# Edge numbers transposed on TensorE instead of scattered by DMA, and a last group of one chunk, in a four-layer graph kernel

## The chip, the cores and the metric

The kernel runs on one core of one Trainium2 chip. The metric is device time in microseconds (us). It is one launch that computes four graph layers over the same 3125 nodes and 53125 edges. The engines are PE (TensorE), DVE (VectorE), ACT (ScalarE), POOL (GpSimd) and SP (SyncE); each works through its own instructions in order and waits on semaphores. SP issues nearly all the plain DMAs, POOL the indirect ones (gathers of rows by an index list).

## The reference, cut to what matters

```python
# x: (3125, 256); src, dst: (53125,) int32, sorted by dst; edge_weight: (53125,)
x = layernorm(x + relu(segment_sum(norm * (x @ W0)[src], dst) + b0))            # layer 0
x = layernorm(x + segment_sum(w * x[src], dst) @ Wrel.T + b + x @ Wroot.T)      # layer 1
z = einsum('nd,hdf->nhf', x, W)                                                 # layer 2, 4 heads of 64
es, ed = (z * a_src).sum(-1), (z * a_dst).sum(-1)
e = leaky_relu(es[src] + ed[dst], 0.01);  e = where(e == 0, -1000, e)
m = segment_max(e, dst);  ex = exp(e - m[dst]);  alpha = ex / segment_sum(ex, dst)[dst]
x = layernorm(x + segment_sum(alpha[:, :, None] * z[src], dst).reshape(N, 256))
x = layernorm(x + relu(segment_sum(w * (x @ W3)[src], dst) + b3))               # layer 3
```

The change concerns how layer 2 reads `src` and `dst`. Both are 212.5 KB lists of integers in memory.

## The kernel before, in words

**Layers 0, 1 and 3** work by tiles of 128 nodes (25 tiles). For 16 of them ("dense") a weighted adjacency matrix is built from one-hot matrices and multiplied on PE; for the other 9 ("sparse") POOL gathers source rows and PE scatters them. To find the edges of a tile, the kernel writes an edge list to memory (`tab` to `flat`, L464), and from it a table `etab` of overlapping rows of 128 edges (L474, 4983 KB); POOL gathers 32 of these rows per dense tile (`edge_rows`, L642, into `raw`).

**Layer 2** works by groups of 640 consecutive edges: 128 partitions times KC = 5 chunks. There are 84 groups; 83 are full, and the last has 5 edges. For each group POOL issues 5 indirect DMAs, each gathering 128 rows of `ztab` by the indices `idx[:, g, c]` (L706). DVE builds the one-hot of destinations from `dstf[:, g, c]`, forms the logits, maxima and exponents with ACT, and PE sums prob times rows in 4 heads times 5 chunks (L1872, 20 matmuls, which the profile shows as 40). The groups form a software pipeline: in one iteration g DVE takes logits of g+1, maxima of g and rescales g-2; PE sums group g-1.

**The edge layout in layer 2.** Partition p of group g holds the 5 consecutive edges 640g + 5p to 640g + 5p + 4. So loading `dst` to `dst_i[p, g, k]` (L470) and copying `src` to `source_nodes[p, g, k]` in memory (L475) go in pieces of 5 integers (20 bytes): 128 times 83 of them each. The last group has 1 partition with 5 edges; its other partitions get node 0 from a small zeroed tile `spare` (L478) and a destination of 1e30 (L922).

**The order of work at the start.** SP issues from one instruction stream: the first edge loads (L445 to L447, which wait for DVE's clearing memsets through s_pad), x, the weights, the edge list, three padded copies of the lists, then the destinations (L470, L472), `etab` (L474, after the edge list), the sources (L475 to L478), the 25 tiles of layer 0's rows in five stores (L482, each behind five tiles of the loop below), and then the index lists of the first sparse blocks (L502). DVE meanwhile makes digit one-hots (L1002, L1003) that PE counts (L1523) into degrees (L1061), and after that DVE, ACT and PE run **the x loop**: 25 tiles, each turned on PE (L1550), copied by ACT (L734), multiplied (L1558), scaled by ACT (L729), split in bf16 parts by DVE and ACT (L1093, L745, L1086). At tile 23 DVE first needs the gathered `raw` rows (L992). After the loop DVE makes the first one-hots of layer 0 (L1118 to L1126), then waits for the list of destinations of the first sparse block (L1179), and adds the first weights (L1139); from there on the layers run as one long chain.

POOL waits for `etab`, gathers `raw` (L642), clears two tiles by memset (L667), and goes on with the gathers of layer 0.

Of the kernel before, what the change touches and what calls it, by code (L numbers as in the profile page):

```python
# [7 lines left out]
ALU = mybir.AluOpType  # L8
# [31 lines left out]
NOWHERE = 4095  # L40
WIDE = 18
# [6 lines left out]
def gnn_program(nc, x, src, dst, edge_weight, w0, b0, w_rel, b_rel, w_root, w_att, att, w3, b3, out):  # L48
# [6 lines left out]
    REST = (E - FULL * EP * KC) // KC  # L55
# [8 lines left out]
    assert FULL * EP * KC + REST * KC == E and 0 < REST < EP  # L64
# [73 lines left out]
    landed_between = [16 * KC * len(range(s, GROUPS, SLOTS)) for s in range(SLOTS)]  # L138
# [7 lines left out]
    with ctx:  # L146
# [48 lines left out]
        spare = sb("spare", [EP, KC], I32)  # L195
# [29 lines left out]
        def carver(whole):  # L225
# [38 lines left out]
        dst_i = carve(EP, FULL + 1, KC, dt=I32)  # L264
# [11 lines left out]
        ybuf = big2[:, 0:2 * NPAD].rearrange("p (t f) -> p t f", f=D)  # L276
        aw = [big2[:, (2 + j) * NPAD:(3 + j) * NPAD].rearrange("p (b d) -> p b d", b=NT) for j in range(2)]
# [69 lines left out]
        sparse1_banks, sparse3_banks = banks[2:4], banks[0:2]  # L347
        granules = banks[7][0:1, 3 * NPAN:3 * NPAN + NT]
# [91 lines left out]
        def _(sp):  # L440
# [276 lines left out]
        def _(act):  # L717
# [53 lines left out]
            for h in range(2):  # L771
                digits(0, h, first=True)
# [742 lines left out]
        def _(pe):  # L1515
# [447 lines left out]
```

## Time and profile before

| | us |
|---|---|
| median of 3 runs (1622.21 to 1625.48) | 1622.26 |
| the profiled execution's own time | 1624.98 |
| its span on the core | 1623.2 |
| PE busy | 1440.8 (89%) |
| DVE busy | 1172.5 (72%) |
| POOL busy | 900.7 (55%) |
| ACT busy | 487.2 (30%) |

The span is some 1.8 us shorter than the execution's own time, which holds what lies around it. The page also gives the chain of waits that ended last: PE has 48% of it, POOL 16%, "issue" 12%, DVE 9%, DMA 9%, SP's queue 3%. Two of its entries lie in one stretch at the start (the table `edge_rows` and the gather from it), and POOL's 15% is layer 2, where L706 issues 420 gathers. In the timeline a row has its start, its length, the engine and line, the tiles out<-in, and in brackets the idle time before it and who ended that.

### The profile page before, as it was taken

How to read it: one execution, taken by the hardware profiler on the slowest of the kernel's cores; microseconds unless marked ns; L12 is line 12 of the kernel's file. 1: busy time of each engine (PE TensorE's matmuls, PEld its weight loads, DVE VectorE, ACT ScalarE, POOL GpSimd, SP SyncE). 2: the span in 40 equal slices, each digit the busy share in tenths (PEclk: the TensorE clock that was granted, in tenths of full speed). 3: DMA queues.
4: the chain of work that ended last, by engine and by line, in shares of the span. 5: the costliest groups of instructions: out<-in, count | busy, mean ns of one | idle time of the engine just before them, and what ended most of it. 6: DMA issues, size and time to landing. Idle time of an engine off the chain costs nothing.

```text
span 1623.2 us, 36636 instructions
## 1 busy us (share of the span) xinstructions
PE 1440.8 (89%) x12043; PEld 1162.8 (72%) x12043; DVE 1172.5 (72%) x3011; ACT 487.2 (30%) x907; POOL 900.7 (55%) x913
## 2 busy tenths in 40 slices
PE   4949999999998999999588898888888879999998
PEld 4738777877776888887366666666666657888887
DVE  9768888888863344345599999999999969443433
ACT  0522222222210111013355545455555546100000
POOL 0126455554454556563677777777777710456774
PEclk9969999999999999999599999999899969999999
DMA  8975545445565565541344444444444441766652
GB/s 203 109 155 173 166 163 181 143 163 165 195 218 208 183 200 189 171 142 47 94 111 112 114 111 112 112 114 111 113 113 111 112 138 66 262 209 226 199 152 80
DMA packets 132296, 241.49 MB, mean 149 GB/s; under 512 B 70299, under 2 KB 94975, under 8 KB 125967
## 3 DMA queue, kind: packets, MB, share of 16 engines
q0 software_dynamic: 45024, 128.68, 28.3%
q1 hardware_dynamic: 87087, 110.47, 22.9%
q8 instruction: 100, 1.64, 0.4%
q14 instruction: 85, 0.70, 0.1%
HBM read 193.42 MB, written 50.96 MB: 151 GB/s over the span
## 4 chain that ended last, share of the span: by engine, by line
PE 48%; POOL 16%; issue 12%; DVE 9%; DMA 9%; SPq 3%; ACT 1%; DVEq 1%; POOLq 0%
PE bank L1740 15%; POOL ring L706 15%; PE bank L1622 7%; PE bank L1688 7%; PE bank L1614 3%; PE bank L1667 3%; PE bank L1872 3%; PE bank L1640 3%; DMA edge_rows<-edge_list 2%; DMA ring<-attention_rows,work 2%; DMA big<-rows_layer,big 2%; PE bank L1749 2%; POOL big L661 1%; PE bank L1607 1%; DMA ring<-edge_rows,ring 1%
## 5 line engine op out<-in xcount | busy, mean ns | idle before, releaser
L706 POOL DMA_INDIRECT ring<-attention_rows,work x420 | 399.6, 951 | 150.4 <-issue 146.4
L661 POOL DMA_INDIRECT big<-rows_layer,big x304 | 289.6, 953 | 265.9 <-issue 241.2
L657 POOL DMA_INDIRECT ring<-rows_layer,ring x152 | 149.9, 986 | 181.7 <-PE bank L1667 131.7
L1872 PE MATMUL bank<-work,ring 128*65 128x48 f32 x3360 | 239.8, 232 | 9.3 <-ACT work L874 8.6
L1872 PEld LDWEIGHTS bank<-work,ring 128*65 128x65 f32 x3360 | 228.9, 148 | 18.2 <-ACT work L874 16.8
L874 ACT ACTIVATE work<-work 128x960 f32<-128x960 f32 x84 | 161.6, 1924 | 84.3 <-DVE work L1419 83.6
L1740 PE MATMUL bank<-big,ring 128*128 128x256 f32 x750 | 164.2, 379 | 0.0
L1740 PEld LDWEIGHTS bank<-big,ring 128*128 128x128 f32 x750 | 142.5, 190 | 19.5
L1740 PE MATMUL bank<-big 128*128 128x256 f32 x664 | 145.9, 379 | 0.0
L1688 PE MATMUL bank<-big 128*128 128x256 f32 x608 | 139.2, 383 | 7.4 <-DMA big<-rows_layer,big 7.2
L1740 PEld LDWEIGHTS bank<-big 128*128 128x128 f32 x664 | 126.1, 190 | 17.7 <-ACT big L898 0.4
L1622 PE MATMUL bank<-big 128*128 128x256 bf16 x1200 | 133.8, 273 | 0.6
L1688 PEld LDWEIGHTS bank<-big 128*128 128x128 f32 x608 | 114.0, 192 | 26.2 <-DMA big<-rows_layer,big 10.1
L1855 PE MATMUL bank<-ident 128*32 128x512 bf16 x420 | 130.4, 411 | 0.0
L1622 PEld LDWEIGHTS bank<-big 128*128 128x128 bf16 x1200 | 116.1, 98 | 16.2 <-ACT big L758 3.0
L1847 PEld LDWEIGHTS bank<-ident,work 96*128 96x128 f32 x336 | 46.4, 199 | 108.3 <-DVE work L1400 104.1
L1847 PE MATMUL bank<-ident,work 96*128 96x96 f32 x336 | 60.5, 305 | 65.0 <-DVE work L1400 64.4
L763 ACT ACTIVATE std<-mv,epsc 128x1 f32<-128x1 f32 x100 | 29.4, 294 | 288.8 <-DVE mv L1145 286.4
L1386 DVE TENSOR_TENSOR work<-work,bank 128x960 f32<-128x960 f32 x84 | 96.1, 1144 | 0.9 <-issue 0.8
L1126 DVE TENSOR_TENSOR work<-work,ring 128x1600 bf16<-128x1600 bf16 x102 | 96.1, 983 | 0.0
L1394 DVE TENSOR_REDUCE work<-work 128x192 f32<-128x960 f32 x84 | 96.0, 1143 | 0.0
L1419 DVE TENSOR_TENSOR work<-work,bank 128x960 f32<-128x960 f32 x84 | 95.8, 1141 | 0.0
(254 smaller groups left out, 2290.5 us busy)
## 6 DMA issues: line engine op xcount, KB each, us to landing
adjacency<-big SPq DMA_DIRECT2D x16, 1600.0 KB, 6.4
big<-adjacency SPq DMA_DIRECT2D x16, 1600.0 KB, 8.0
ring<-adjacency SPq DMA_DIRECT2D x16, 1600.0 KB
ring<-attention_rows,work POOLq DMA_INDIRECT x420
rows_layer<-big SPq DMA_DIRECT2D x50, 128.0 KB, 2.2
edge_rows<-edge_list SPq DMA_DIRECT2D x1, 4983.0 KB
big<-rows_layer,big POOLq DMA_INDIRECT x304, 2.9
rows_layer<-big SPq DMA_DIRECT2D x5, 960.0 KB, 10.8
```

Source lines behind the costliest of these rows:

```text
L657: G.indirect_dma_start(out=rows0[:, s, :], out_offset=None, in_=y0tab[:, :], in_offset=bass.IndirectOffsetOnAxis(ap=src_l0[j][:, c:c + 1], ...
L661: G.indirect_dma_start(out=rows1[:, s, :], out_offset=None, in_=(y1tab if q < 2 * LAYER else y3tab)[:, :], in_offset=bass.IndirectOffsetOn ...
L706: G.indirect_dma_start(out=rows[0:EP, s, c, 0:ZG], out_offset=None, in_=ztab[:, :], in_offset=bass.IndirectOffsetOnAxis(ap=idx[:, g, c:c + ...
L874: S.activation(prob[:, k % 2, :, :], val[:, k % 3].rearrange("p a c -> p c a"), ACT.Exp).then_inc(y["prob_ready"], 1)
L1126: ins = V.tensor_tensor(oh[h][2][:, j], oh[h][1], repeated(digs[h][:, W1 + j], NT * PAN), ALU.mult)
L1386: V.tensor_tensor(val[:, k % 3].rearrange("p (h w) c -> p h w c", h=H), pen[:, k % 3].unsqueeze(1).to_broadcast([EP, H, WIN, KC]), lg.rear ...
L1622: ins = mm(dense_bank[:, 0:D], ac[:, b, :], y0p[:, b, j, :], start=False, stop=False, skip_group_check=True)
L1688: mm(bank[:, 0:D], hot1[:, q % 2, c, :], rows1[:, s, :], start=False, stop=False, skip_group_check=True).then_inc(chunk_done, 1)
L1740: ins = mm(bank[:, 0:D], slots[s][:, b, :], ybuf[:, b, :], start=(b == 0), stop=(b == NT - 1), skip_group_check=True)
L1847: ins = mm(mb_bank[:, j * 2 * WIN:(j + 1) * 2 * WIN], mg[:, j:j + 1].to_broadcast([2 * WIN, P]), ident[0:2 * WIN, 0:2 * WIN], start=True, ...
L1855: mm(bank[0:32, :].rearrange("p (a b) -> p a b", a=4), ident16[:, 0:32], columns, start=True, stop=True, skip_group_check=True)
L1872: ins = mm(sum_banks[k % 3][0:FH, h * WIN:(h + 1) * WIN], rows[0:EP, s, c, h * FH:(h + 1) * FH], prob[:, k % 2, c, h * WIN:(h + 1) * WIN], ...
```

## The change

Sources and destinations are loaded with one group per partition: `dst_g` and `src_g` are 84 partitions of 640 consecutive edges (pieces of 2560 bytes), lying in the storage that layer 0's output rows take later. ACT casts both to float. PE transposes each in 5 blocks of 84x128 into bank 7, in the x loop's steps 4 (destinations) and 9 (sources). ACT copies the turned destinations to `dstf` in its step 4; DVE casts the turned sources to integers (`src_t`) in its step 13; SP stores `src_t` to `source_nodes` behind a wait for that. Edge c*128 + p of a group is now in chunk c and partition p. With that order the last group's 5 edges are all in chunk 0, so POOL gathers one chunk for it and PE sums one chunk. Some semaphores of the count phase are merged, and padded destinations are 2^24 in place of 1e30.

```diff
+            for a, d in ((dst_g, dst), (src_g, src)):
+                sp.dma_start(a[0:FULL, :], d[0:FULL * EP * KC].rearrange("(g e) -> g e", g=FULL)).then_inc(ld_dsti, 16)
+                sp.dma_start(a[FULL:GROUPS, 0:REST], d[FULL * EP * KC:E].rearrange("(g e) -> g e", g=1)).then_inc(ld_dsti, 16)
             sp.wait_ge(s_tab, 6)
             sp.dma_start(flat[0:P * COLS, :].rearrange("(p e) f -> p e f", p=P), tab[:]).then_inc(s_flat, 16)
...
-            sp.dma_start(dst_i[:, 0:FULL, :], dst[0:FULL * EP * KC].rearrange("(g p k) -> p g k", p=EP, k=KC)).then_inc(
-                ld_dsti, 16)
-            sp.dma_start(dst_i[0:REST, FULL, :], dst[FULL * EP * KC:E].rearrange("(p k) -> p k", k=KC)).then_inc(ld_dsti, 16)
             sp.wait_ge(s_flat, 32)
             sp.dma_start(etab[:, :], bass.AP(flat.tensor, 0, [[GRAN * FIELDS, ROWS + 1], [1, P * FIELDS]])).then_inc(s_etab, 16)
-            sp.dma_start(src_all[:, 0:FULL, :], src[0:FULL * EP * KC].rearrange("(g p k) -> p g k", p=EP, k=KC)).then_inc(
-                s_srcs, 16)
-            sp.dma_start(src_all[0:REST, FULL, :], src[FULL * EP * KC:E].rearrange("(p k) -> p k", k=KC)).then_inc(s_srcs, 16)
-            sp.dma_start(src_all[REST:EP, FULL, :], spare[REST:EP, :]).then_inc(s_srcs, 16)
+            sp.wait_ge(s_srct, 1)
+            sp.dma_start(src_all, src_t).then_inc(s_srcs, 16)
...
@@ POOL, layer 2
-                    for c in range(KC):
+                    for c in range(chunks_of(g)):
@@ ACT, before the degrees, and in its x loop
+            act.wait_ge(ld_dsti, 64)
+            S.copy(dst_gf, dst_g).then_inc(s_grows, 1)
+            S.copy(src_gf, src_g).then_inc(s_grows, 1)
...
+                if t == 4:
+                    act.wait_ge(s_gturn, 1)
+                    S.copy(dstf[:].rearrange("p g c -> p c g"), turned_numbers).then_inc(s_grows, 1)
...
@@ DVE, clearing at the start (before s_pad), and in its x loop
-            V.memset(spare[:], 0)
+            V.memset(dst_g[GROUPS // 32 * 32:GROUPS, :], FAR_NODE)
+            V.memset(src_g[GROUPS // 32 * 32:GROUPS, :], 0)
...
-            dve.wait_ge(ld_dsti, 32)
-            V.tensor_copy(dstf[:, 0:FULL, :], dst_i[:, 0:FULL, :])
-            link(V.tensor_copy(dstf[0:REST, FULL, :], dst_i[0:REST, FULL, :]))
...
+                if t == 13:
+                    dve.wait_ge(s_gturn, 2)
+                    V.tensor_copy(src_t.rearrange("p g c -> p c g"), turned_numbers).then_inc(s_srct, 1)
@@ PE, x loop and layer 2
+            def turn_numbers(of, ready):
+                pe.wait_ge(s_grows, ready)
+                for c in range(KC):
+                    ins = T(turned_numbers[:, c, :], of[:, c * EP:(c + 1) * EP], ident[0:GROUPS, 0:GROUPS])
+                ins.then_inc(s_gturn, 1)
...
+                if t == 4:
+                    pe.wait_ge(s_cur, 1)
+                    turn_numbers(dst_gf, 1)
+                elif t == 9:
+                    turn_numbers(src_gf, 3)
...
-                        for c in range(KC):
+                        for c in range(chunks_of(k)):
```

SP's stream before, from the edge list to layer 0's rows (`edge_rows` is `etab`, `rows_layer` the rows of layer 0, `big` on-chip storage):

```order
L464 DMA edge_list<-big 128x2496 [waits s_tab]
L465 DMA edge_list<-big 1x96
L470 DMA big<-in_dst 128x83x5
L472 DMA big<-in_dst 1x5
L474 DMA edge_rows<-edge_list 3322x768 [waits s_flat]
L475 DMA source_nodes<-in_src 128x83x5
L477 DMA source_nodes<-in_src 5x1
L478 DMA source_nodes<-spare 127x5
L482 DMA rows_layer<-big 128x5x768 [waits b_p3] x5
```

(The six padded copies, L468 and L469, stand between L465 and L470.) The same stretch now:

```order
L476 DMA big<-in_dst 83x640
L477 DMA big<-in_dst 1x5
L476 DMA big<-in_src 83x640
L477 DMA big<-in_src 1x5
L479 DMA edge_list<-big 128x2496 [waits s_tab]
L480 DMA edge_list<-big 1x96
L486 DMA edge_rows<-edge_list 3322x768 [waits s_flat]
L488 DMA source_nodes<-big 128x420 [waits s_srct]
L492 DMA rows_layer<-big 128x5x768 [waits b_p3] x5
```

The two loads moved ahead of the edge list, and the store of the sources stands alone behind `edge_rows`, with a wait.

PE's stream at the x loop's steps 3 to 5 before (`x_sb` is turned to banks 1 and 6, the products go to banks 4 and 5):

```order
L1550 MATMUL bank1<-ident,x_sb 128x128 [waits b_xTc]
L1550 MATMUL bank1<-ident,x_sb 128x128
L1558 MATMUL bank5<-ring,xnT 128x256 [waits b_r1,b_xTc]
L1558 MATMUL bank5<-ring,xnT 128x256
L1550 MATMUL bank6<-ident,x_sb 128x128 [waits b_xTc]
L1550 MATMUL bank6<-ident,x_sb 128x128
```

and now:

```order
L1568 MATMUL bank1<-ident,x_sb 128x128 [waits b_xTc]
L1568 MATMUL bank1<-ident,x_sb 128x128
L1576 MATMUL bank5<-ring,xnT 128x256 [waits b_r1,b_xTc]
L1576 MATMUL bank5<-ring,xnT 128x256
L1598 MATMUL bank7<-ident,big2 128x84 [waits s_grows,s_cur]
L1598 MATMUL bank7<-ident,big2 128x84 x4
L1568 MATMUL bank6<-ident,x_sb 128x128 [waits b_xTc]
L1568 MATMUL bank6<-ident,x_sb 128x128
```

Five transposes of the numbers stand between a product and the next turn of x; the sources' five stand in the same way five steps later.

## Rows read from the trace of the kernel before

**Rows 1.** Timeline, SP's DMA queue: start, length (us), line.
```profile
26.86 7.51 SPq L472 DMA_DIRECT2D big<-in_dst  x1
...
36.13 12.83 SPq L475 DMA_DIRECT2D source_nodes<-in_src  x1
49.00 40.83 SPq L477 DMA_DIRECT2D source_nodes<-in_src  x1
...
90.34 10.56 SPq L482 DMA_DIRECT2D rows_layer<-big  x5
103.36 0.39 SPq L502 DMA_DIRECT2D ring<-edge_sources  x1
```
**Rows 2.** The chain that ended last, from the start: start, length, what.
```profile
34.41 39.85 DMA edge_rows<-edge_list
...
75.31 19.95 DMA ring<-edge_rows,ring
```
**Rows 3.** Waits, 0 to 130 us: total us, times, longest.
```profile
DVE ring L992 <- DMA ring<-edge_rows,ring: 7.1, 1, 7.1
...
DVE deg L1061 <- PE bank L1523: 2.6, 1, 2.6
...
DVE ring L1179 <- DMA ring<-edge_destinations: 2.5, 1, 2.5
```
**Rows 4.** Timeline, DVE at the start, a clearing memset and the first work.
```profile
1.28 0.41 DVE L915 MEMSET big<- 32x417 int32 x1
...
5.79 0.38 DVE L940 TENSOR_SCALAR big<-big 128x416 int32<-128x416 int32 x1 [0.90 <-DMA big<-in_dst]
```
**Rows 5.** Windows in the x loop: us, busy per engine, clock, DMA share, GB/s.
```profile
64.00:74.00 10.00, 9.82 (x51) 7.70 (x49) 8.27 (x21) 8.70 (x26) 0.00 (x0) 1.00 1.40 14
```
**Rows 6.** Timeline, 56 to 82 us, durations of kinds of work.
```profile
56.00 1.09 PE L1575 MATMUL bank<-ident,ring 128*128 128x128 f32 x8
59.42 0.38 PE L1550 MATMUL bank<-ident,x_sb 128*128 128x128 f32 x2
65.08 0.68 DVE L1078 COPY w_rr<-bank 128x512 f32<-128x512 f32 x1
72.29 0.28 DVE L1068 COPY wz<-ring 128x256 f32<-128x256 f32 x1
76.33 5.48 POOL L667 MEMSET big<- 128x3200 f32 x2
77.31 0.42 DVE L1086 TENSOR_TENSOR big<-work,big 128x256 bf16<-128x256 f32 x1
80.32 1.65 DVE L1068 COPY wz<-ring 128x256 f32<-128x256 f32 x1
```
**Rows 7.** Timeline, the end of layer 2.
```profile
1304.18 0.95 POOL L706 DMA_INDIRECT ring<-attention_rows,work  x1 [0.30 <-issue]
1306.79 0.42 PE L1838 MATMUL bank<-ident,work 128*96 128x128 f32 x2
1309.47 0.18 DVE L1366 TENSOR_TENSOR work<-ring,bank 128x20 f32<-128x20 f32 x1 [3.08 <-DMA ring<-attention_rows,work]
1311.01 4.57 PE L1872 MATMUL bank<-work,ring 128*65 128x48 f32 x40
1317.09 0.42 DVE L1400 TENSOR_REDUCE work<-bank 96x2 f32<-96x256 f32 x1 [1.96 <-PE bank L1838]
1318.26 2.52 PE L1872 MATMUL bank<-work,ring 128*65 128x48 f32 x40
1322.45 3.62 PE L1872 MATMUL bank<-work,ring 128*65 128x48 f32 x40 [1.68 <-ACT work L874]
```
**Rows 8.** DMA issues: KB each, median us from issue to landing.
```profile
rows_layer<-big SPq DMA_DIRECT2D x5, 960.0 KB, 10.8
```
**Rows 9.** Windows, for the granted clock (third figure from the right).
```profile
112.00:120.00 8.00, 7.02 (x93) 6.69 (x94) 5.42 (x12) 2.81 (x7) 5.92 (x7) 0.58 0.43 125
...
1310.00:1312.00 2.00, 1.95 (x14) 1.95 (x14) 1.82 (x6) 0.00 (x0) 0.00 (x0) 0.50 0.01 4
```

More of the change, by code:

```diff
@@ L40 @@
 NOWHERE = 4095
+FAR_NODE = 1 << 24
 WIDE = 18
@@ L54, in gnn_program @@
     GROUPS = FULL + 1
-    REST = (E - FULL * EP * KC) // KC
+    REST = E - FULL * EP * KC
+    LAST_CHUNKS = -(-REST // EP)
     NT = -(-N // P)
@@ L63, in gnn_program @@
     MOST = -(-ROWS // (P // GRAN)) + 1
-    assert FULL * EP * KC + REST * KC == E and 0 < REST < EP
+    assert 0 < REST < EP * KC and GROUPS * KC <= 512
     assert GROUPS > 2 * SLOTS and SLOTS % 2 and NPAD - N >= WIN and D == 2 * P
@@ L137, in gnn_program @@
     landed_before = [landings(2 * TEN - SLOTS + s, 2) for s in range(SLOTS)]
-    landed_between = [16 * KC * len(range(s, GROUPS, SLOTS)) for s in range(SLOTS)]
+    landed_between = [16 * sum(KC if g < FULL else LAST_CHUNKS for g in range(s, GROUPS, SLOTS)) for s in range(SLOTS)]
     def list_loads(q):
@@ L276, in gnn_program @@
         ybuf = big2[:, 0:2 * NPAD].rearrange("p (t f) -> p t f", f=D)
+        carve = carver(big2)
+        dst_g = carve(GROUPS, KC * EP, dt=I32)
+        src_g = carve(GROUPS, KC * EP, dt=I32)
+        dst_gf = carve(GROUPS, KC * EP)
+        src_gf = carve(GROUPS, KC * EP)
+        src_t = carve(EP, GROUPS, KC, dt=I32)
         aw = [big2[:, (2 + j) * NPAD:(3 + j) * NPAD].rearrange("p (b d) -> p b d", b=NT) for j in range(2)]
@@ L358, in gnn_program @@
         s_digits, s_dup = sem("s_digits"), sem("s_dup")
-        s_gq, s_hist, s_histc, s_hT, s_colsum, s_colsumc, s_first, s_cur, s_nswb = (
-            sem(f"s_{n}") for n in ("gq", "hist", "histc", "hT", "colsum", "colsumc", "first", "cur", "nswb"))
-        s_srcs = sem("s_srcs")
+        s_gq, s_totals, s_totals_read, s_cur, s_nswb = (sem(f"s_{n}") for n in ("gq", "totals", "totals_read", "cur", "nswb"))
+        s_srcs, s_srct, s_grows, s_gturn = sem("s_srcs"), sem("s_srct"), sem("s_grows"), sem("s_gturn")
         s_tab, s_flat, s_etab = sem("s_tab"), sem("s_flat"), sem("s_etab")
-        s_gm, s_gmT, s_dg, s_bb, s_sweeps = (sem(f"s_{n}") for n in ("gm", "gmT", "dg", "bb", "sweeps"))
+        s_ranges, s_ranges_spread, s_sweeps = sem("s_ranges"), sem("s_ranges_spread"), sem("s_sweeps")
         s_onehots, s_cnt, s_deg, s_sqd, s_dinv = (sem(f"s_{n}") for n in ("onehots", "cnt", "deg", "sqd", "dinv"))
@@ L404, in has, with chunks_of, landed_rows @@
             return 0 <= g < GROUPS
+        def chunks_of(g):
+            return KC if g < FULL else LAST_CHUNKS
+        def landed_rows(r, g):
+            return r * landed_between[g % SLOTS] + 16 * (KC * (g // SLOTS) + chunks_of(g))
         def uses(r, g):
@@ L551, in _ @@
             sp.sem_inc(held, 1)
-            sp.wait_ge(s_srcs, 48)
+            sp.wait_ge(s_srcs, 16)
             sp.dma_start(idx, src_all).then_inc(idx_ready, 16)
@@ L772, in _ @@
                 digits(0, h, first=True)
+            act.wait_ge(s_srcs, 16)
             def rows_of_layer1(m):
@@ L921, in _ @@
             V.memset(pad_w, 0.0).then_inc(s_pad, 1)
-            link(V.memset(dstf[:, FULL:, :], BIG))
             V.memset(epsc[:], EPS)
@@ L1025, in _ @@
             link(V.tensor_scalar(rounds, rounds, float(P // GRAN), None, ALU.mult))
-            V.tensor_reduce(most[:], banks[7][0:1, 2 * NPAN:3 * NPAN], AX_X, ALU.max).then_inc(s_colsumc, 1)
-            dve.wait_ge(s_colsumc, 1)
+            V.tensor_reduce(most[:], banks[7][0:1, 2 * NPAN:3 * NPAN], AX_X, ALU.max).then_inc(s_totals_read, 1)
+            dve.wait_ge(s_totals_read, 2)
             link(V.tensor_tensor(most[:], most[:], unsorted[0:1, :], ALU.max))
@@ L1363, in logits_sum @@
                 def logits_sum(k):
-                    dve.wait_ge(gathered[k % SLOTS], 16 * KC * uses(r, k) + nswb * landed_before[k % SLOTS])
+                    dve.wait_ge(gathered[k % SLOTS], landed_rows(r, k) + nswb * landed_before[k % SLOTS])
                     dve.wait_ge(y["lg"], 5 * number(k) + 6)
```

43 lines of the change are left out of this document (21 added, 22 removed).

## The prediction

> **What bounds the kernel now.** I read the page's chain of waits first, then its pieces in order of time, because the change acts at two places only: the first 115 us and the last 25 us of layer 2. At the start the chain runs through SP's issues, then through the transfer that makes `edge_rows` (39.85 us) and the gather from it (19.95 us) [rows 2]. SP's queue shows why they are so long: the issue of the piecewise load of the destinations held SP 7.51 us, and the piecewise copy of the sources 12.83 and 40.83 us, until 89.83 [rows 1]. They are 128 x 83 pieces of 20 bytes each, issued around `edge_rows`, and the gather by POOL shares the DMA engines with them.
>
> What that costs is not 54 us. The table of waits gives what DVE lost by it: 7.1 us at L992 for the gathered rows, in the x loop's tile 23, and 2.5 us at L1179 for the first list of destinations [rows 3]. Everything else of the backlog lies beside DVE, ACT and PE, which work on counts and on the x loop until then. In the x loop PE is busy 9.82 of 10 us, ACT 8.70 and DVE 8.27 [rows 5]: the three are a ring with little room, and work put into it is paid nearly in full.
>
> In layer 2 POOL issues gathers without a pause, 0.95 us each and 0.30 between them, 1.25 us a chunk [rows 7]. DVE waits a little for each group. For the last group it waits 3.08 us, from 1306.39 [rows 7], since that group's five gathers ended at 1305.13. Behind it the pipeline drains: two groups of sums on PE, and the last one, with nothing beside it, 3.62 us.
>
> **The start, what goes.** (1) The wait of 7.1 us at L992. Now `edge_rows` has no pieces ahead of it or behind it. Even if its transfer took the old 39.85 us and the gather the old 19.95, counted from an issue some 5 us earlier (7.51 us of issue gone, about 2.5 added), they would end near 90, about when DVE arrives; without the pieces they end tens of microseconds earlier. I take all 7.1.
>
> (2) The wait of 2.5 us at L1179. SP issued the list at 103.36 because it had only come to the five stores of layer 0's rows at 90.34 and needed 10.56 us to issue them [rows 1], 960 KB each, which landed 10.8 us after issue [rows 8] with the list behind them. Now SP is free for the stores as the x loop delivers tiles, at tile 14, 15, 20 and 25, so one store is left at the end. The lists are then issued 2.5 us behind it (103.36 less 100.90), around 96. DVE has the 9 to 10 us of one-hots to do after its loop, so the list has landed. I take all 2.5.
>
> (3) POOL's two memsets (5.48 us from 76.33) lay in the x loop. DVE's copy L1068 took 1.65 us where its twin took 0.28, and ended with them; the sum L1086 beside them took its usual 0.42 [rows 6]. POOL comes to the memsets as soon as `raw` is gathered, now near 47, so the copy is free again: 1.37 us less. (The Trainium skill, "SBUF — State Buffer", section "Who interferes with whom", says that VectorE's two-port copies and a GpSimd instruction exclude one another for their whole length, while an operation with two on-chip inputs is held up only by a GpSimd instruction that reads. This trace agrees: 1.65 against 0.28, and 0.42 unchanged.)
>
> Together 10.97 us.
>
> **The start, what comes.** (4) Two memsets of 640 integers per partition before s_pad. At 0.41 us for 416 [rows 4] that is 0.63 each, 1.26 us. SP's first load waits for them, and DVE idled 0.90 us for that load's data [rows 4], so the delay goes into the path: +1.26. (5) PE's 2 x 5 transposes. Eight of 128x128 took 1.09 us, 0.136 each, and two of `x_sb` 0.38, 0.19 each [rows 6]; an 84-column one is no longer. From below PE might hide them in its 0.18 us of idle per 10, so nearly nothing; I take 10 x 0.136 = 1.36, bounds 0 and 1.9. (6) ACT's copy of 420 turned numbers, and DVE's cast of 420. The nearest row is 0.68 us for 512 from the same kind of bank [rows 6], so 0.56 each; between 0 (room in the ring) and 0.68. I take 1.12. (7) ACT's two casts of the untransposed numbers and the new loads lie in ACT's idle time before the degrees: nothing, if the loads are there by then (below, the rival that ends slower). (8) The two DVE casts into `dstf` go, but DVE waited 2.6 us for PE right behind them [rows 3]: nothing. (9) SP's new wait for DVE's step 13 has the store of the sources and all five row stores behind it. The first two of these come up to eight tiles later than they could, still some 20 us ahead of where they were; POOL's gathers need the last store only: nothing.
>
> (The Trainium skill, "TensorE: Matmul & The Clock Gate", Part 4 on the transpose mode, gives about 275 ns for a 128x128 bf16 transpose in a kernel. Ten of these would be an estimate of 2.75 us and take 1.4 us from the gain. The trace here has 0.136 to 0.19 for fp32, and the measurement decides.)
>
> Sum of costs 1.26 + 1.36 + 1.12 = 3.74; the start gains 10.97 - 3.74 = 7.2 us. Bounds: costs from 1.26 to 1.26 + 1.9 + 1.36 = 4.5, so 6.5 to 9.7. From there on all layers are one chain, and the whole is shifted.
>
> **The end of layer 2.** (10) The last group gathers once, so its data is there 4 x 1.25 = 5 us earlier, near 1304.4, and DVE does not wait at L1366. It could go on at 1306.39. But the next instruction, the group maximum, needs PE's L1838, which ended at 1307.21; it began about 0.1 us after L1366's 1309.47. So 1309.58 less 1307.25, 2.3 us, are gained; at most 3.08. (11) The sums at 1311.01 ran at a granted clock of 0.50 [rows 9], the lower level of 1.2 GHz, and took 4.57 us where the next 40 matmuls took 2.52 [rows 7]. By this the transposes came late and DVE waited 1.96 us at L1400 [rows 7]. PE is idle 2.3 us less ahead of them, and whether the clock is high then I can't tell: 0 to 1.96, I take 1.0. (12) The last group's sums are 4 matmuls in place of 20, 8 of the 40 in the row: 8/40 x 3.62 = 0.72, at the low clock 8/40 x 4.57 = 0.91. With nothing beside them 2.7 us go; at most 2.9.
>
> Together 2.3 + 1.0 + 2.7 = 6.0 us, bounds 5.0 and 7.9. The DVE and ACT work of the last group keeps its size.
>
> **Sum.** 7.2 + 6.0 = 13.2 us. The profiled execution took 1624.98 us, its span 1623.2, so it would take 1611.8 with a span near 1610.0. Against the median of the runs shown, 1622.26, that is 1609.1; I say 1609. The bounds alone give gains of 11.5 to 17.6, 1604.7 to 1610.8.
>
> **Rivals.**
>
> A. The memsets hit DVE at their new place. Near 47 to 53 DVE makes one-hots, which PE's counts and the degrees wait for. For it: L1068. Against it: L1086 with two inputs was untouched. If each waited as L1068 did, up to 5.48 us come back: 13.2 - 5.5 = 7.7, 1614.5.
>
> B. The end of layer 2 is bound by PE's and DVE's own drain. The wait at L1366 becomes one for PE, the low clock stays, and of (10) and (11) nothing is left: 7.2 + 2.7 = 9.9, 1612.4. Against it: L1838 was done at 1307.21.
>
> C. The clock is up where it was low. From 112 to 120 PE was busy 7.02 us at a mean granted clock of 0.58 [rows 9]; at full clock that work takes 4.1, so up to 2.9 us. With shorter idle stretches of PE before it, and the full 1.96 of (11), the gain is 13.2 + 2.9 + 1.0 = 17.1, 1605. Against it: PE still has about 5 us of nothing while DVE makes the first one-hots.
>
> D. Slower than before. ACT takes its instructions in order, and its two casts wait for all four new loads before it may take the square root of the degrees, near 56.5 (PE's work behind the last count starts at 56.00 [rows 6]). Nothing of the x loop starts without it. Each microsecond that the loads land after that is one lost. If they landed as late as `edge_rows` did, at 74.3 [rows 2], the loss is 17.8, less the 13.2: 1622.26 + 4.6 = 1626.9. It decides from 56.5, and outweighs the gains from about 70. For it: a load queued behind 3 MB of x and the weights. Against it: 84 pieces of 2560 bytes, ahead of the edge list, not behind it.
>
> E. The change doesn't do what it says: the gather is late by itself, for instance since `edge_rows`, 3322 rows of overlapping reads, is what takes long, or the list waits for SP all the same. By (1) even the old durations leave little of the wait; but if both waits stayed, the start would lose 3.74 - 1.37 = 2.4 us, and with the 6.0 of layer 2's end the whole gain would be 3.6; with the low bound of 5.0 there it is 2.6, no change by measurement: 1619.7.
>
> **How the numbers follow.** My forecast 0.66; A 0.10; B 0.08; C 0.10; D 0.03; E 0.03. A change of 0.2%, 3.2 us, is about what a measurement of this kernel can tell from none. Faster than that are the forecast, A, B and C: 0.94; E is the same, 0.03; D is slower, 0.03. The range goes from C with the top of its bounds, 1602.5, to A, 1614.5; the forecast's own is 1604.7 to 1610.8.
>
> **What the profile after would show.** SP's queue with no issue over 2 us between `edge_rows` and the row stores; L992's and L1179's successors without a wait on a DMA; the memsets near 47 and one-hots of 0.57 and 0.68 us beside them; both copies to `wz` near 0.28 us; five transposes in two places of the x loop with 0.7 us each; SP's first load near 4.2 us. At the end of layer 2, 416 gathers, no wait for their data in the last group, and 8 records of sums instead of 40 under 1 us. The forecast is wrong if ACT's square root or DVE's L1061 starts much later than 57.5, if DVE's one-hots lengthen, or if the gain at 115 us is given back before 700 us.

## The result, and the profile after

The changed kernel took 1611.85 us (median of 4, 1609.19 to 1612.43), the kernel before 1623.87 on the same chip (4, 1622.21 to 1625.51): a ratio of 0.9923, 95% interval 0.9909 to 0.9938, so 12.0 us faster. Its profiled execution has a span of 1610.6 us, 12.6 less than before. The time lies in the wide range (1602.5 to 1614.5), 2.85 us above the value of 1609, and 1.05 above the forecast's own bounds, which end at 1610.8. Of the 2.85 us, 1.6 are the kernel before's, which has 1623.87 here and 1622.26 in the forecast. The gain lies inside the 11.5 to 17.6 us of the bounds, 1.2 below the sum of 13.2. That it comes so near is partly luck: the start gave less than its sum, layer 2 more, and the two nearly cancel.

Both waits of DVE are gone. These are DVE's first lines in the changed kernel's table of waits, 0 to 125 us; L992 is now L1010 and L1179 is L1197, and neither is in the table [rows 3]:

```profile
DVE work L1108 <- ACT big L742: 6.7, 13, 0.9
DVE deg L1076 <- PE bank L1542: 2.8, 1, 2.8
```

SP's queue, against [rows 1]:

```profile
24.33 0.29 SPq L476 DMA_DIRECT2D big<-in_dst  x1
...
27.03 8.66 SPq L477 DMA_DIRECT2D big<-in_src  x1
35.74 0.73 SPq L479 DMA_DIRECT2D edge_list<-big  x1
36.52 0.81 SPq L480 DMA_DIRECT2D edge_list<-big  x1
...
47.97 0.91 SPq L486 DMA_DIRECT2D edge_rows<-edge_list  x1
79.54 0.34 SPq L488 DMA_DIRECT2D source_nodes<-big  x1
79.92 15.32 SPq L492 DMA_DIRECT2D rows_layer<-big  x5
98.09 0.37 SPq L512 DMA_DIRECT2D ring<-edge_sources  x1
```

The issues of 12.83 and 40.83 us have gone, but `edge_rows` was issued at 47.97, not before 34.41 as I expected. Two things made it late. The issues of the four new loads held SP from 24.33 to 35.74, 11.4 us; 8.66 of them are the load of five numbers that stands behind the 83 rows of the sources. (The 7.51 us at L472 in [rows 1] are such a small load too, behind the pieces; the issue of the pieces themselves, L470, took 0.50.) Then SP waited from 42.2 to 47.97 for the edge list. What both wait for is in the DMA line of the stretch 20 to 50 us, 0.75 us a digit (busy tenths, then GB/s):

```profile
DMA  9998267584541000000010499674401000000104
GB/s 321 308 273 171 87 209 242 105 93 44 86 86 68 27 24 27 27 24 24 27 46 24 197 420 363 219 270 151 178 24 35 27 24 24 27 27 25 41 19 43
```

From about 30 to 36 us and again from 42 on the queue moves mostly 24 to 27 GB/s, with a busy share of a tenth or less. From 31 to 35 us the DMA view has this:

```profile
DMA packets 40, 0.10 MB, mean 26 GB/s; under 512 B 0, under 2 KB 0, under 8 KB 40
q1 hardware_dynamic: 40, 0.10, 6.5%
```

Each of these packets is one row of 2560 bytes, ten go in a microsecond, and 6.5% of 16 engines is one engine. So the two new loads of 83 rows pass through one DMA engine; the packets in the trace run from 28.88 to 45.63 us. The edge list, issued behind them, needs that engine too: 120 of its 128 rows had started by 38.44 us, the other eight started from 45.75 to 47.07. ACT's cast shows when they were there, and POOL's and DVE's rows what followed:

```profile
46.41 0.72 ACT L733 CAST big<-big 84x640 f32<-84x640 int32 x1 [37.34 <-DMA big<-in_src]
```
```profile
70.39 1.02 POOL L652 DMA_INDIRECT ring<-edge_rows,ring  x1 [67.16 <-issue]
71.41 5.49 POOL L677 MEMSET big<- 128x3200 f32 x2
```
```profile
7.39 0.38 DVE L958 TENSOR_SCALAR big<-big 128x416 int32<-128x416 int32 x1 [1.32 <-DMA big<-in_dst]
57.65 0.37 DVE L1076 TENSOR_SCALAR deg<-bank 64x25 f32<-64x25 f32 x2 [2.84 <-PE bank L1542]
74.85 2.19 DVE L1083 COPY wz<-ring 128x256 f32<-128x256 f32 x1
78.60 0.91 DVE L1115 CAST big<-bank 128x420 int32<-128x420 f32 x1
94.77 0.15 DVE L1120 COPY unsorted<-epsc 128x1 f32<-128x1 f32 x1
105.61 0.23 DVE L1197 TENSOR_SCALAR ring<-ring 128x10 bf16<-128x10 int32 x1
106.62 1.17 DVE L1157 SCALAR_TENSOR_TENSOR big<-big,ring,bank 128x400 f32<-128x400 f32 x2
```

So the memsets are still in the x loop, and still hold a copy: 2.19 us where its twin took 0.28. In the kernel before, the degrees and the first weighted sum (L1139, now L1157) were these rows:

```profile
56.18 0.37 DVE L1061 TENSOR_SCALAR deg<-bank 64x25 f32<-64x25 f32 x2 [2.62 <-PE bank L1523]
...
112.30 1.17 DVE L1139 SCALAR_TENSOR_TENSOR big<-big,ring,bank 128x400 f32<-128x400 f32 x2
```

The sum starts at 106.62 instead of 112.30: the start gained 5.68 us.

The end of layer 2, against [rows 7]:

```profile
1294.19 0.95 POOL L716 DMA_INDIRECT ring<-attention_rows,work  x1 [0.31 <-issue]
1301.31 0.16 DVE L1385 TENSOR_TENSOR work<-ring,bank 128x20 f32<-128x20 f32 x1
1303.02 2.56 PE L1901 MATMUL bank<-work,ring 128*65 128x48 f32 x40 [0.47 <-ACT work L892]
1306.63 0.41 DVE L1419 TENSOR_REDUCE work<-bank 96x2 f32<-96x256 f32 x1
1311.99 0.67 PE L1901 MATMUL bank<-work,ring 128*65 128x48 f32 x8 [0.96 <-ACT work L892]
1312.77 0.35 DVE L1459 TENSOR_TENSOR big<-big,bank 65x192 f32 x1 [0.74 <-PE bank L1901]
```

No wait for data, 2.56 us where the sums took 4.57, and 8 matmuls at the end. From the last gather of the last full group (one gather before 1294.19, so 1292.94; before it was five earlier, 1297.91) to DVE's last addition it is now 19.83 us. Before, it was 28.28 us, up to this row:

```profile
1326.19 0.35 DVE L1440 TENSOR_TENSOR big<-big,bank 65x192 f32 x1 [4.28 <-PE bank L1872]
```

That is 8.45 us gained. I call this stretch the tail.

### The profile page after: what moved, and what is told of

It is laid out like the page before. It is cut to its first block, busy times and chain, and to the rows that moved or that the text cites. A ratio compares the mean times of both kernels' runs of the same rounds, so it can differ in the third digit from the quotient of the medians.

```text
span 1610.6 us, 36607 instructions
## 1 busy us (share of the span) xinstructions
PE 1435.2 (89%) x12021; PEld 1158.3 (72%) x12021; DVE 1173.5 (73%) x3010; ACT 489.2 (30%) x910; POOL 903.0 (56%) x909
## 4 chain that ended last, share of the span: by engine, by line
PE 46%; POOL 19%; issue 14%; DVE 11%; DMA 6%; ACT 1%; DVEq 1%; SPq 1%; POOLq 0%; ACTq 0%
POOL ring L716 16%; PE bank L1769 13%; PE bank L1651 8%; PE bank L1717 5%; PE bank L1696 3%; PE bank L1643 3%; POOL big L671 3%; PE bank L1669 3%; DMA big<-rows_layer,big 2%; PE bank L1901 2%; PE bank L1636 1%; PE bank L1778 1%; DMA ring<-attention_rows,work 1%; DMA big<-edge_weights 1%; PE bank L1576 1%
## 5 line engine op out<-in xcount | busy, mean ns | idle before, releaser
L716 POOL DMA_INDIRECT ring<-attention_rows,work x416 | 394.5, 948 | 147.6 <-issue 143.3
L1901 PE MATMUL bank<-work,ring 128*65 128x48 f32 x3328 | 235.3, 231 | 12.2 <-ACT work L892 11.6
L1901 PEld LDWEIGHTS bank<-work,ring 128*65 128x65 f32 x3328 | 224.4, 146 | 21.1 <-ACT work L892 18.5
L652 POOL DMA_INDIRECT ring<-edge_rows,ring x17 | 48.2, 2837 | 91.5 <-issue 71.7
L1405 DVE TENSOR_TENSOR work<-work,bank 128x960 f32<-128x960 f32 x84 | 96.1, 1144 | 0.5 <-ACT work L892 0.2
L1512 DVE TENSOR_TENSOR u<-bank,bias 128x256 f32<-128x256 f32 x25 | 10.6, 424 | 117.4 <-PE bank L1769 92.3
```

The source lines that it names most:

```text
L716: G.indirect_dma_start(out=rows[0:EP, s, c, 0:ZG], out_offset=None, in_=ztab[:, :], in_offset=bass.IndirectOffsetOnAxis(ap=idx[:, g, c:c + ...
L1405: V.tensor_tensor(val[:, k % 3].rearrange("p (h w) c -> p h w c", h=H), pen[:, k % 3].unsqueeze(1).to_broadcast([EP, H, WIN, KC]), lg.rear ...
L1901: ins = mm(sum_banks[k % 3][0:FH, h * WIN:(h + 1) * WIN], rows[0:EP, s, c, h * FH:(h + 1) * FH], prob[:, k % 2, c, h * WIN:(h + 1) * WIN], ...
```

## The experiments

All are edits of the changed kernel. The table puts their readings side by side: the median against the kernel before on the same chip; the start of the degrees (L1076); the stretch from there to the end of the x loop (L1120); how long the copy into `wz` took that met POOL's memsets; the start of the first weighted sum. Times in us. The line numbers are the changed kernel's; in the variants they lie a few lines off. The ratio is estimated from all the runs, and differs from the quotient of the two medians by up to 0.0007.

| run | median / before | ratio, 95% | degrees | x loop | copy | first sum |
|---|---|---|---|---|---|---|
| before | | | 56.18 | 41.52 (34.42 without the wait) | 1.65 | 112.30 |
| changed | 1611.85 / 1623.87 | 0.9923, 0.9909–0.9938 | 57.65 | 37.12 | 2.19 | 106.62 |
| e0_again | 1610.01 / 1624.14 | 0.9910, 0.9896–0.9924 | 57.19 | 37.42 | 2.48 | 106.45 |
| e0_third | 1613.14 / 1628.14 | 0.9905, 0.9889–0.9921 | 57.11 | 39.86 | 4.13 | 108.81 |
| e1 split loads | 1608.27 / 1624.14 | 0.9900, 0.9884–0.9915 | 58.41 | 34.16 | 0.28 | 104.42 |
| e2 last group five | 1617.79 / 1624.14 | 0.9960, 0.9945–0.9975 | 57.64 | 37.15 | 2.06 | 106.64 |
| e4 turned later | 1613.34 / 1624.14 | 0.9933, 0.9919–0.9948 | 57.97 | 38.10 | 4.20 | 107.92 |
| e8 = e1 + e4 | 1606.89 / 1622.63 | 0.9906, 0.9892–0.9919 | 58.16 | 33.07 | 0.29 | 103.08 |
| e5 = e1 + later padding | 1606.32 / 1622.63 | 0.9906, 0.9893–0.9918 | 56.04 | 34.16 | 0.28 | 102.06 |
| e7 all three | 1606.12 / 1622.63 | 0.9895, 0.9880–0.9911 | 56.30 | 33.08 | 0.28 | 101.23 |
| e7_again | 1606.69 / 1628.14 | 0.9864, 0.9848–0.9881 | 56.49 | 33.07 | 0.28 | 101.41 |
| e6 = e1 + pieces | 1615.40 / 1622.63 | 0.9958, 0.9944–0.9971 | 58.81 | 37.90 | 2.02 | 111.64 |
| e10 early memsets | 1606.98 / 1628.14 | 0.9870, 0.9853–0.9887 | 59.37 | 34.16 | 0.28 | 105.39 |
| e3 rows and sums | 1608.81 / 1628.14 | 0.9883, 0.9866–0.9900 | 57.53 | 34.17 | 0.28 | 103.56 |

**e0_again, e0_third: the changed kernel as yardstick.**

> The changed kernel once more, on the chip that the next three runs share, as their yardstick. Both theories below expect what the result showed: a gain of 11 to 14 us on the kernel before, SP's issue of edge_rows near 48 us, the one copy into wz beside POOL's memsets at about 2.2 us.

> The changed kernel again, as yardstick for the other runs of this chip: 11 to 14 us faster than the kernel before.

By the medians they gained 14.1 and 15.0 us, a little more than the 11 to 14 that I expected. What they teach is the copy: 2.19, 2.48 and 4.13 us in three profiles of one kernel. It lasts until POOL's memsets end. DVE comes to it some tenths earlier or later, and in e0_third POOL came to its memsets 1.4 us later (72.79 for 71.41).

**e1_split: the loads of 83 rows in two.**

```diff
-  sp.dma_start(a[0:FULL, :], d[0:FULL * EP * KC].rearrange("(g e) -> g e", g=FULL)).then_inc(ld_dsti, 16)
+  for lo, hi in ((0, 80), (80, FULL)):
+      sp.dma_start(a[lo:hi, :], d[lo * EP * KC:hi * EP * KC].rearrange("(g e) -> g e", g=hi - lo)).then_inc(ld_dsti, 16)
```

(ACT waits for all six loads in place of four; that line is left out here.)

> Only the two 83-row loads of the untransposed numbers are split into rows 0 to 79 and rows 80 to 82. Theory S (the loads are slow because 83 rows were not spread over the DMA engines, and the edge list's small piece stands behind them): the 80-row loads are done within 3 us of their issue, ACT's first cast of them starts before 31 us instead of at 46.4, SP issues edge_rows before 40 us instead of at 48.0, so the gather into raw and POOL's memsets start at least 8 us earlier and end before 69 us, outside the stretch in which DVE copies into wz; both wz copies take 0.28 us and the kernel gains 1.5 to 2.2 us on the changed kernel. Rival B (the queue is late by the bytes ahead of these loads): ACT's cast still starts at 45 us or later, edge_rows is issued at 47 or later, and the time is the changed kernel's within 0.5 us. Rival M (the memsets cost as much beside the one-hots or the counts): edge_rows early, but the x loop begins later than in the changed kernel, with no net gain.

Theory S came out, but for one size: the loads were not done 3 us after their issue. They were issued from 24.20 to 26.26, their rows moved from 28.46 to 31.20, and ACT's cast started at 31.83, not before 31:

```profile
31.83 0.72 ACT L734 CAST big<-big 84x640 f32<-84x640 int32 x1 [22.76 <-DMA big<-in_src]
```

The cast is 14.6 us earlier. The issues of the loads held SP for 2.1 us in place of 11.4, and it issued `edge_rows` at 33.73 and not 47.97; the gather into `raw` started at 57.49, 12.9 us earlier, the memsets ended at 64.0, and both copies took 0.28. The x loop was 2.96 us shorter for a copy that was 1.91 us shorter. The degrees started 0.76 us later, which the casts and the loads do not explain (see the last section); 2.2 us are left at the first weighted sum, and the median is 1.7 below that of e0_again. Rival B's late cast did not come, nor rival M's loss.

**e10_early_memsets: the memsets ahead of the wait for edge_rows.**

```diff
   pool.wait_ge(s_cur, 1)
+  for j in range(2):
+      G.memset(aw[j], 0.0).then_inc(c_zero, 1)
   pool.wait_ge(s_etab, 16)
```

(The two lines behind `edge_rows(0)` that cleared the same buffers are gone.)

> The changed kernel with one edit: POOL clears the two buffers before it waits for edge_rows, so near 46 to 52 us, beside DVE's one-hots, and not behind the gather. Theory K (the copy into wz that the memsets held for 2.19 us cost more than its 1.9, since PE stood idle by it and its clock then fell to 0.66 for four us): the degrees start where they did, 57.6 within 0.4, the one-hots beside the memsets keep their 0.67 and 0.57 us, both copies take 0.28, the stretch from the degrees to the end of the x loop falls from 37.1 to about 34.2, and DVE's first weighted sum comes at 103.7 instead of 106.6. Rival A of the prediction (the memsets hold the one-hots): the degrees come 3 to 5.5 us later and the whole is not faster than the changed kernel.

The memsets ran from 45.44 to 50.91, and beside them DVE's one-hots kept their length:

```profile
47.95 0.69 DVE L1020 TENSOR_TENSOR work<-ring,big 128x1024 bf16<-128x1024 bf16 x1
48.56 0.57 DVE L1021 TENSOR_TENSOR work<-ring,big 128x800 bf16<-128x800 bf16 x1
```

The x loop was 34.16 us, as theory K has it. DVE ran up to the degrees within 0.25 us of the changed kernel's times, and started them 1.7 us later, after a longer wait for PE (4.5 us for 2.8); so that part of the expectation failed, but it isn't the memsets holding one-hots, rival A's mechanism. By the medians the edit was worth 6.2 us beside e0_third, whose profile had the copy at 4.13. Of these, 3.4 are there at the first weighted sum; where the others come from was not followed.

Why a held copy costs more than its own time is seen in PE's clock (third figure from the right). The changed kernel, then this one:

```profile
78.00:82.00 4.00, 3.17 (x10) 2.53 (x11) 3.43 (x9) 1.71 (x5) 0.00 (x0) 0.66 0.41 140
```
```profile
78.00:82.00 4.00, 3.33 (x17) 2.66 (x17) 3.93 (x11) 2.87 (x9) 0.00 (x0) 1.00 0.46 156
```

PE did 10 instructions instead of 17 in the same 4 us. In PE's own rows of the changed kernel the idle time comes first, then the low clock, at which four products take 1.65 and 1.91 us instead of 1.03 to 1.10:

```profile
75.08 1.10 PE L1576 MATMUL bank<-ring,xnT 128*128 128x256 f32 x4
...
78.83 1.65 PE L1576 MATMUL bank<-ring,xnT 128*128 128x256 f32 x4 [2.43 <-DVE work L1108]
...
80.70 1.91 PE L1576 MATMUL bank<-ring,xnT 128*128 128x256 f32 x4
```

In e0_third the clock was 0.57 from 78 to 82 and 0.58 from 82 to 86. Against the same kernel with free copies (e1, or e8 for e4) the loop grew by more than the copy did in all six profiles that have a held copy (the changed kernel's three, e2, e4, e6): by 1.05 to 1.21 us more in five (e6 without its wait), by 1.85 in e0_third. The kernel before is the check. Its copy was held too, for 1.65 us from 80.32, but its clock stayed at 1.00:

```profile
78.00:82.00 4.00, 3.60 (x18) 2.85 (x18) 3.26 (x7) 3.23 (x10) 3.82 (x2) 1.00 1.38 11
```

Its loop, without the wait, is 1.35 us longer than that of e8 below, which has neither a held copy nor the transposes: the copy's 1.37 and nothing more.

**e4_turned_later and e8_split_turned: the transposes behind the x loop.** PE does both sets behind `turn_fields(0, -1)`, ACT copies both behind its first digits, and SP stores the sources behind the first lists.

```diff
   turn_fields(0, -1)
+  turn_numbers(dst_gf, 1)
+  turn_numbers(src_gf, 3)
```

> The transposes of the numbers leave the x loop: PE does both sets behind the transposes of the first fields, ACT copies both results behind its first digits, and SP's store of the sources moves behind the first lists. PE and ACT have idle time there, while DVE makes the first one-hots. Theory L (in the x loop every us of PE, ACT or DVE is paid): 0.92 (ACT's copy) + 0.91 (DVE's cast) + 1.06 (ten transposes) go, 2 to 2.9 us gained on the changed kernel at DVE's first weighted one-hots. Rival R (the loop's ring had room for them, or ACT's two copies delay the first counts): within 1 us of the changed kernel.

> The split loads together with the later transposes. In the split kernel the stretch from the degrees to the end of the x loop is 34.2 us; before the change it was 41.5 less the wait of 7.1 and the 1.4 of the held copy, 33.1. Theory: the transposes and their two copies cost the difference, 1.1 us, not the 2.5 predicted; with them out of the loop it is 33.1 again, and both copies into wz take 0.28. DVE's first weighted sum starts at 103.3. Rival (they cost their full 2.5 to 2.9 us, and the split kernel hid it by something else): the stretch is 31.3 to 31.7 us.

e4 says nothing on its question, and neither its theory nor its rival came out: the first weighted sum is 1.3 us later than in the changed kernel, and the median 3.3 us above that of e0_again. DVE reached the copy into `wz` 0.8 us earlier, POOL the memsets 1.2 us later, the copy was held 4.20 us, and the loop grew to 38.10. I had not reckoned with that. e8 has no such copy, and there the loop fell from 34.16 (e1) to 33.07. The ten transposes with their copy and cast cost 1.09 us there. In the whole time it does not show: e8 is 15.7 us below the kernel before, e1 15.9.

**e5_split_pads: DVE's padding after s_pad.** The two memsets of the new buffers stand behind the one that raises s_pad, and SP waits for them ahead of the new loads only.

> The split loads, and DVE makes the padding of the two new buffers after s_pad, so SP's first load of the edges does not wait for it. Theory (the two memsets of 640 integers are on the path at their full 1.26 us): SP's first load goes out 1.3 us earlier, DVE's first instruction on the destinations starts near 6.1 us instead of 7.4, the degrees at 57.1 instead of 58.4, and DVE's first weighted sum at 103.1 instead of 104.4; -1.3 us on the split kernel. Rival (the path to the degrees has its own floor in PE's counts and ACT): the degrees start within 0.4 us of the split kernel's.

SP's first load went out at 2.77 instead of 4.30, DVE's first instruction on the destinations started at 6.03 instead of 7.39, and the degrees at 56.04, in e7 at 56.30 and 56.49; the ten profiles with the padding ahead of s_pad have 57.11 to 59.37. The least difference is 0.6, that to e1 2.37; the two memsets took 0.59 us each, 1.3 us with the step between them. The theory holds, and not the rival; but its size at the degrees lies within a scatter that is PE's, and in the whole time (16.3 us below the kernel before, e1 15.9) the 1.3 us are not shown.

**e7_all_three, e7_again.**

> The split loads, the later transposes and the later padding together. If the three add up: 1.7 (split) + 1.1 (transposes) + 1.3 (padding) = 4.1 us less than the changed kernel, about 1606 as a median, DVE's first weighted sum near 102.0 us. If they don't: the ring of PE, ACT and DVE or the low clock behind the first one-hots takes some back, and the time stays within 1 us of the split kernel.

> The kernel with all three edits again, beside the changed kernel on the same chip. Theory: at DVE's first weighted sum it is 5.4 us ahead of the changed kernel, at 101.2, and 2 to 3 us of that are given back to the low clock behind the first one-hots; the time is 3 to 5 us below the changed kernel's. Rival (the ends of both differ by the clock's chance alone): under 2 us.

At the first weighted sum the three add up: 5.4 and 5.2 us ahead of the changed kernel. On the chip that ran both, the medians are 1606.69 and 1613.14, 6.5 us apart and more than expected, since e0_third has the worst copy of the three. By the medians this is the fastest version, but e5 (0.2 us behind it on its chip), e8 (0.8) and e10 (0.3 behind e7_again) are as fast within the intervals. e10 shows that a lead at the start isn't kept in full: at the first weighted sum it is 4.0 us behind e7_again, at layer 2's first gather 0.3 (769.69 and 769.42).

**e6_pieces: one copy in 20-byte pieces put back.**

```diff
+  sp.dma_start(pieces[:, 0:FULL, :], src[0:FULL*EP*KC].rearrange("(g p k) -> p g k", p=EP, k=KC))
   sp.wait_ge(s_srct, 1)
```

> The split loads, and behind edge_rows one copy of 128 x 83 pieces of 20 bytes of the sources into a buffer that nobody reads, as the kernel before had it. Theory W (the two waits of DVE, 7.1 for the gathered rows and 2.5 for the first list, came from the pieces): SP's issue of the pieces takes about 40 us from 34.7 on, the gather into raw starts later than 70 us instead of at 57.5, SP comes to the row stores within 1 us of where it did or later than 78, and DVE waits for the gathered rows or for the first list, 3 us or more in all; the kernel loses 4 to 10 us of the split kernel's time. Rival (the gather was late because edge_rows itself takes long, or because POOL came late to it): the gather starts within 3 us of 57.5, DVE has neither wait, and the time is the split kernel's within 1 us.

Both waits of DVE came back, the second one whole, the first in part:

```profile
DVE ring L1203 <- DMA ring<-edge_destinations: 2.8, 1, 2.8
...
DVE ring L1016 <- DMA ring<-edge_rows,ring: 0.9, 1, 0.9
```

The gather into `raw` started at 71.38 instead of 57.49, the memsets hit the copy again (2.02), and the first weighted sum was 7.2 us late: 3.7 in the two waits, 1.7 in the copy, 0.4 at the degrees and 1.4 in the rest of the loop and behind it. The median is 7.2 us below the kernel before, where e1 has 15.9, so 8.6 us were lost, in the 4 to 10 that I expected. One step went otherwise than said: the issue of the pieces held SP 13.49 us, not 40; the 40 of [rows 1] were those of a small transfer queued behind them, and here SP waited for DVE's step at that time. At the index lists SP was still 6.8 us late, by 6.67 us for issuing the store of the sources.

**e2_last_five: the last group gathers and sums five chunks.** `chunks_of(g)` gives KC for every group.

> The changed kernel, but the last group gathers and sums five chunks as before; four of them hold padding. Theory T (the last group's size gave all of layer 2's extra gain, 8.5 us behind the last gather of the group before it, by an earlier start, a full clock and fewer sums): the stretch from layer 2's first gather to its end is 8 to 9 us longer than in the changed kernel, the sums before the last run at a low clock again, time +8 to +9 us. Rival P (part of it is a faster gather pace that has nothing to do with the last group): +5.5 to +7 us, the span of the first 415 gathers unchanged at 520.0 us.

The end of layer 2 is that of the kernel before again (POOL's last gather, DVE, PE):

```profile
1295.62 0.95 POOL L716 DMA_INDIRECT ring<-attention_rows,work  x1 [0.30 <-issue]
```
```profile
1301.04 0.18 DVE L1385 TENSOR_TENSOR work<-ring,bank 128x20 f32<-128x20 f32 x1 [3.19 <-DMA ring<-attention_rows,work]
1308.75 0.42 DVE L1419 TENSOR_REDUCE work<-bank 96x2 f32<-96x256 f32 x1 [2.04 <-PE bank L1867]
1317.76 0.35 DVE L1459 TENSOR_TENSOR big<-big,bank 65x192 f32 x1 [4.21 <-PE bank L1901]
```
```profile
1302.58 4.57 PE L1901 MATMUL bank<-work,ring 128*65 128x48 f32 x40
```

The tail is 1317.76 less 1289.37, 28.39 us, against 19.83 and 19.84 in the changed kernel's profiles, so theory T has the tail right; the median is 7.8 us above that of e0_again, between T's 8 to 9 and rival P's 5.5 to 7. The gathers up to the last full group took 518.89 us, as in the changed kernel (518.76), where the kernel before took 520.09: that 1.3 us is not the last group's. The other profiles have 518.1 to 519.6, and there is one profile of the kernel before, so some of it can be scatter.

**e3_rows_and_sums: one gather and five sums; 82 and 81 rows.**

> Two edits at places far apart. At the end of layer 2 the last group gathers one chunk but sums five on PE (the four others meet weights of zero). From the last gather of the group before it to DVE's last addition the kernel before took 28.3 us and the changed one 19.8. Theory (the fewer sums are a term of their own): 16 more matmuls for each pair of heads' records, 2.4 to 2.9 us, so 22.2 to 22.8 us. Rival (the sums lie beside DVE's and ACT's work): under 21 us. At the start the two loads are split otherwise: the destinations as rows 0 to 81 and row 82, the sources as rows 0 to 80 and rows 81, 82. Theory R (a load of n rows is served by as many DMA engines as the largest divisor of n up to 16: 83 gives one, 82 two, 81 nine, 80 sixteen): the 82 rows take about half of the 8.3 us that one engine needs for 83, 4.1 us, the 81 rows about 1 us; ACT's first cast starts 3 to 5 us after the start of the 80-row kernel's, near 35 us. Rival F (rows are dealt over all engines and only the odd remainder goes to one): the cast starts within 1 us of the 80-row kernel's 31.8.

The tail is 22.44 us (1307.29 less 1284.85), so the needless sums of four empty chunks cost 2.6 of the 8.45. The cast of the destinations and sources began at 35.28, 3.5 us behind e1, as theory R says, and not within 1 us, as rival F does. The rows of the loads end at 34.43 in this trace. From 33.5 to 34.5 us:

```profile
DMA packets 132, 0.09 MB, mean 89 GB/s; under 512 B 94, under 2 KB 112, under 8 KB 132
```

The 20 packets between 2 and 8 KB are 19 rows of 2560 bytes and one of the edge list: twice the ten a microsecond of the 83 rows, so two engines.

## Why the prediction was right, and where it was not

**(1), (2): right.** Both waits went in full, 9.6 us, and with one set of pieces e6 brings 3.7 us of them back (0.9 for the gathered rows, 2.8 for the list). But (1) had a false support. From the real issue at 47.97 the old durations would have ended at 107.8 and not near 90, and the wait would have stayed. It went because they shrank, which (1) says too: the gather into `raw` began 22.4 us after the issue of `edge_rows`, before 40.9 us (34.41 to 75.31), and DVE used the rows at 92.3 without a wait.

**(3): failed.** The memsets did not leave the x loop. The step that failed is the one before it: "counted from an issue some 5 us earlier (7.51 us of issue gone, about 2.5 added)". The issue came 13.6 us later, the gather into `raw` at 70.39, and the memsets at 71.41 and not near 47. The new loads added 11.4 us of issue in place of 2.5, and the wait for the edge list 5.8 more. I had looked at how many bytes the new loads bring and where they stand in the queue, and not at 83 rows on one engine, with the small loads and eight rows of the edge list behind them. In place of a gain of 1.37 the copy took 0.54 us more than before, and the clock took a further 1.05 (2.96 of the loop less the copy's 1.91): 1.59 us lost, 2.96 from what I had said. e1, e3 and e10 remove it in two ways.

**(4): right in size.** 1.6 us at DVE's first use of the destinations, 1.47 at the degrees, for 1.26; the figure at the degrees lies within their scatter.

**(5), (6): too high.** 1.09 us for 2.48. The single prices were off in both directions: five transposes took 0.53 us together, 0.11 each and not 0.136, the copy and the cast 0.92 and 0.91, not 0.56. But the ring of PE, ACT and DVE was not as full as I read from PE's 9.82 of 10 us [rows 5].

**(7) to (9) and rival D.** ACT's casts ended near 47.8, ten microseconds ahead of the degrees; nothing was lost. SP's new wait ended at 79.54, the lists were issued at 98.09 (I had said around 96), and DVE used them at 105.61 without a wait. D was closer than I made it, and by its own mechanism, loads that land late.

**The start in sum.** 9.6 less 1.47 (degrees), less 2.70 (the loop, 37.12 for 34.42: 1.09 + 1.59 and rounding), and 0.25 more between the loop and the sum: 5.68, for a predicted 7.2. With (3) in working order, in e1, it was 7.88.

**(10) to (12): the mechanism right, the sizes low.** From the last full group's last gather to L1385 (before L1366): 11.56 to 8.37, 3.2 us for (10)'s 2.3. I had held it back for PE's transposes at 1306.79; they were not in the way. From that group's maximum (L1419, before L1400) to the next such instruction: 7.51 (1309.58 to 1317.09) to 5.24 (1301.39 to 1306.63), 2.3 us for (11)'s 1.0, since the clock stayed at 1.00 (from 1298 to 1313 us) and DVE's wait for PE went. From there to the last addition: 9.10 to 6.14, 3.0 us for (12)'s 2.7. Together 8.45 for 6.0; e3 shows 2.6 of it alone. The 1.3 us of the gathers' pace was in no step, and its cause stays open. The sums behind the last full group ran at a clock of 0.50 in the kernel before and in e2; why it is 1.00 in the changed kernel was not tested by itself.

**What was given back.** Rival C was half right: the granted clock was 1.00 from 110 on, before it was 0.50 until 118, and the gain was 7.0 us at POOL's fourth gather into `raw` (136.82 for 143.85). By the next it was 5.3. This row is of the changed kernel, where the kernel before has 1.00:

```profile
145.00:150.00 5.00, 5.00 (x44) 4.03 (x43) 2.36 (x6) 0.70 (x3) 2.35 (x3) 0.75 0.15 44
```

From 158 to 432 us the lead stood at 5.3 to 5.5, and at the first gather of layer 2 at 3.64 (774.18 for 777.82). In e0_again it was 5.9 there, in e0_third 1.1, in e2 7.3. From 432 to 500 us the three profiles of the changed kernel have a clock of 0.97, e2 and the kernel before 1.00; so low stretches fall differently in each execution, and I take them for most of this scatter, some 2 us either way. That they make all of it is not shown. So "the whole is shifted" did not hold, and one sign of being wrong, a gain at 115 us that is given back before 700, came in part. 3.64 and layer 2's 9.8 make 13.4 us at the end of layer 2 against a sum of 13.2: right in total by luck, because the start gave 3.6 less and layer 2 3.8 more than predicted. Behind layer 2 another 0.8 us went, to the 12.6 of the spans; that was not followed.

**Rivals and range.** A fell with e10. B's time, 1612.4, is nearer the measured 1611.85 than the forecast, but its mechanism did not occur: L1385 had no wait, and the clock was 1.00. D and E did not occur. The range's lower end, 1602.5, does not follow from the terms: the top of the bounds, 17.6, and C's 2.9 from 1622.26 give 1601.8.

## What to carry to other kernels

Small pieces cost less in what they move than in what stands behind them: look for the first consumer that waits, and for the queue's next issue. A whole-row load is not cheap by being whole: choose a row count that the DMA engines can share (80 here, not 83), and check the queue's GB/s and packets as well as the length of the next issue. And a stall in a full loop is to be priced with the clock behind it, 2.96 us here for a copy held 1.91.

## What the runs showed of the hardware that was not expected

**Rows and engines.** A load of 83 rows of 2560 bytes moved ten rows a microsecond (26 GB/s), one of 82 rows 19 from 33.5 to 34.5 us in e3, and with 80 rows all 166 rows of both loads moved in 2.8 us. That fits as many engines as the largest divisor of the row count up to 16; other counts were not tried alone. What comes behind on the slow engine waits as well: the edge list's last eight rows moved 7.3 us after its others.

**PE's pace at the start.** PE ran its first products of the x loop at about half pace while the granted clock read 1.00. Of the changed kernel:

```profile
53.18 2.08 PE L1576 MATMUL bank<-ring,xnT 128*128 128x256 f32 x4
55.19 0.75 PE L1542 MATMUL bank<-work 128*64 128x50 bf16 x16
55.87 1.13 PE L1576 MATMUL bank<-ring,xnT 128*128 128x256 f32 x4
```

and of e10, with the window over it:

```profile
56.27 2.08 PE L1576 MATMUL bank<-ring,xnT 128*128 128x256 f32 x4
```
```profile
56.00:58.00 2.00, 2.00 (x11) 1.39 (x9) 0.00 (x0) 0.00 (x0) 0.00 (x0) 1.00 0.73 276
```

Where the pace rises differs between profiles, near 55 us in one and behind 59 in the other with the same DVE times up to there; that is the scatter of the degrees, 57.11 to 59.37. What sets it, and why the granted clock does not show it, stays open.
